# Turning one query block's probabilities with VectorE squares and SBUF transfers in an attention kernel

## What is computed

```
qb = q.reshape(B, H, nb, W, Dh)            # W = 128, nb = 64, H = 16, Dh = 32
kwin = concatenate([kp[:, :, :-2], kp[:, :, 1:-1], kp[:, :, 2:]], axis=3)
vwin = concatenate([vp[:, :, :-2], vp[:, :, 1:-1], vp[:, :, 2:]], axis=3)
scores = einsum('bhnqd,bhnkd->bhnqk', qb, kwin) * scale
scores = where(mask, scores, -1e30)        # |kpos - qpos| <= W and inside the sequence
attn = softmax(scores, axis=-1)
out = einsum('bhnqk,bhnkd->bhnqd', attn, vwin)
return out @ Wout + bout
```

## Time and profile before

| | us |
|---|---|
| median of 3 runs (2625.84 to 2630.6) | 2626.13 |
| the profiled execution | 2629.41 |
| its span, first to last instruction | 2627.6 |
| PE busy in the span | 2576.2 (98%) |
| PE weight loads | 2090.2 (80%) |
| ACT busy | 1638.1 (62%) |
| DVE busy | 1592.0 (61%) |
| POOL busy | 631.8 (24%) |

### The profile page before, as it was taken

The page is one execution under the profiler, slowest core; times in us unless marked ns, Lnnn a source line. Parts: engine busy times, 40 slices in busy tenths (PEclk is TensorE's granted clock), DMA queues, the critical chain, the costliest instruction groups (busy, mean ns, idle before and its releaser), DMA issues.

```text
span 2627.6 us, 55989 instructions
## 1 busy us (share of the span) xinstructions
PE 2576.2 (98%) x19728; PEld 2090.2 (80%) x19728; DVE 1592.0 (61%) x4779; ACT 1638.1 (62%) x4260; POOL 631.8 (24%) x595
## 2 busy tenths in 40 slices
PE   6999999999999999989999999999999999999998
PEld 4888888888888888868888888888888888888885
DVE  5444444444444444357777777777777777777775
ACT  6333333333333333358888888888888888888886
POOL 0011111111111111033333333333333333333332
PEclk7999999999999999999999999999999999999999
DMA  5422222222222222021121111112111111112110
GB/s 181 146 80 81 80 80 80 80 80 80 80 80 80 80 80 64 33 81 34 34 65 34 53 46 42 58 41 58 34 61 39 42 58 42 58 34 65 34 46 29
DMA packets 188361, 167.43 MB, mean 64 GB/s; under 512 B 11328, under 2 KB 143424, under 8 KB 187632
## 3 DMA queue, kind: packets, MB, share of 16 engines
q1 hardware_dynamic: 188000, 164.41, 20.2%
q0 software_dynamic: 144, 0.17, 0.0%
HBM read 97.43 MB, written 67.11 MB: 63 GB/s over the span
## 4 chain that ended last, share of the span: by engine, by line
PE 55%; ACT 1%; issue 0%; DVE 0%; POOL 0%; POOLq 0%; ACTq 0%
PE pT_ps L1193 14%; PE job_ps L1105 14%; PE score_ps L1176 7%; PE job_ps L1123 7%; PE job_ps L1217 7%; PE job_ps L1114 7%; ACT wqkv_raw L928 1%; ACT wqkv_raw L938 0%; PE job_ps L1237 0%; PE score_ps L1227 0%; DVE wqkv_raw L1006 0%; DVE k_lo L1038 0%; ACT q_hi L954 0%; ACT k_hi L957 0%; POOL wout_raw L899 0%
## 5 line engine op out<-in xcount | busy, mean ns | idle before, releaser
L928 ACT ACTIVATE wqkv_raw<-wqkv_raw,neg_max 128x384 f32<-128x384 f32 (+1 forms) x1024 | 633.3, 619 | 186.3 <-DVE neg_max L1006 181.5
L888 POOL TENSOR_SCALAR wqkv_raw<-wqkv_raw,sum_rcp 128x384 f32<-128x384 f32 (+1 forms) x256 | 372.9, 1457 | 960.1 <-DVE sum_rcp L1017 960.1
L494 ACT ACTIVATE relu<-up_ps,fc_scale 128x512 f32<-128x512 f32 x256 | 176.2, 688 | 656.2 <-PE up_ps L625 656.2
L938 ACT COPY wqkv_raw<-pT_ps 128x384 f32<-128x384 f32 (+1 forms) x1024 | 484.7, 474 | 74.4 <-PE pT_ps L1193 74.1
L1193 PE MATMUL pT_ps<-ident,wqkv_raw 128*128 128x128 f32 x3040 | 513.4, 277 | 8.1 <-ACT wqkv_raw L938 7.7
L1006 DVE CUSTOM_DVE_ANT_0 wqkv_raw<-score_ps,mask 128x384 f32<-128x384 f32 (+1 forms) x1024 | 503.5, 548 | 5.7 <-PE score_ps L1176 1.6
L568 DVE SCALAR_TENSOR_TENSOR sq<-up_ps,relu 128x512 f32<-128x512 f32 x256 | 177.0, 692 | 531.8 <-ACT relu L494 530.4
L1193 PEld LDWEIGHTS pT_ps<-ident,wqkv_raw 128*128 128x128 f32 x3040 | 360.0, 140 | 119.1 <-ACT wqkv_raw L938 42.6
L635 PE MATMUL down_ps<-proj_T,sq_hi 128*128 128x512 f32 x1024 | 408.9, 399 | 0.9 <-DVE sq_lo L551 0.9
L637 PE MATMUL down_ps<-proj_T,sq_lo 128*128 128x512 f32 x1024 | 404.3, 395 | 0.0
L621 PE MATMUL up_ps<-f_xT_hi,fc_T 128*128 128x512 f32 x1024 | 399.2, 390 | 1.4 <-DVE low L539 1.4
(11 more groups left out here) (126 smaller groups left out, 4228.2 us busy)
## 6 DMA issues: line engine op xcount, KB each, us to landing
xT_hi<-xT SPq DMA_DIRECT2D x65, 256.0 KB, 3.8
xT_lo<-xT SPq DMA_DIRECT2D x65, 256.0 KB, 4.5
f_x_in<-in_L_attn_x SPq DMA_DIRECT2D x64, 256.0 KB, 3.2
xT<-f_xT_hi SPq DMA_DIRECT2D x64, 256.0 KB, 2.6
xT<-f_xT_lo SPq DMA_DIRECT2D x64, 256.0 KB, 2.8
part_in<-in_L_attn_x SPq DMA_DIRECT2D x64, 256.0 KB, 3.4
partial<-f_y SPq DMA_DIRECT2D x64, 256.0 KB, 2.0
wout_raw<-partial SPq DMA_DIRECT2D x64, 256.0 KB, 2.8
```

The lines of the kernel that those rows point to most:

```text
L888: nc.gpsimd.tensor_scalar(probs[:, u, cols], probs[:, u, cols], sum_rcp[:, u:u + 1], None, ALU.mult).then_inc(last_head_normalised, 1)
L928: nc.scalar.activation(probs[:, u, cols], probs[:, u, cols], ACT.Exp, bias=neg_max[:, u:u + 1], scale=-1.0, accum_out=prob_sum[:, u:u + 1] ...
L938: nc.scalar.copy(pT[:, h, first + seen.start:first + seen.stop, :].rearrange("p w t -> p (w t)"), pT_ps[:, h % 2, seen.start * P:seen.stop ...
```

## The change

For query block 0 of each step the turn leaves PE. Its four heads are scaled by ScalarE (heads 0 and 1) and by GpSimd (heads 2 and 3). VectorE then turns each head by one instruction in 32x32 squares into a new tile `blocks`; a square turned on its own stays in its 32 partitions, so the four strips of 32 partitions have to be carried to where they belong: SP issues 16 transfers SBUF to SBUF a step (4 strips x 4 places), each of 32 partitions x 3 x 128 elements (48 KB in pieces of 512 bytes), into `pT_moved`. `blocks` and `pT_moved` have one buffer each. `probs_times_values` waits for the 16 transfers and multiplies each block on its own, in 24 products of 128 columns where 8 of 256 and 8 of 128 stood. Block 1 goes the old way. To make room, the ring of values has 5 slots (6 before), and that of the attention output 6 steps (8 before). SP's other transfers are issued after the moves of a step.

```diff
+            def move_blocks(t):
+                i, _ = where(t)
+                seen = blocks_seen(i, 0)
+                sp.wait_ge(blocks_turned, HC * (t + 1))
+                if t >= 1:
+                    sp.wait_ge(pv_done, t)
+                for strip in range(STRIPS):
+                    for place in range(STRIPS):
+                        sp.dma_start(pT_moved[place * DH:(place + 1) * DH, seen.start:seen.stop, strip, :, :],
+                                     blocks[strip * DH:(strip + 1) * DH, seen.start:seen.stop, place, :, :]
+                                     ).then_inc(blocks_moved[strip], 16)
...
+            for t in range(STEPS + DC):
+                i, c = where(t)
+                if t < STEPS:
+                    move_blocks(t)
+                if c == 1 and i + XR - 1 < NT:
                     load_x(i + XR - 1)
+                if c >= 2 and i >= 1:
+                    store_y(i - 1, c - 2)
+                    if i < NT:
+                        load_part(i, c - 2)
...
+            def turn_blocks(t, u):
+                i, _ = where(t)
+                seen = blocks_seen(i, 0)
+                if u < HC // 2:
+                    dve.wait_ge(act_heads_normalised, HC // 2 * t + u + 1)
+                else:
+                    dve.wait_ge(pool_heads_normalised, HC // 2 * (t - 1) + u + 1)
+                if u == 0 and t >= 1:
+                    for moved in blocks_moved:
+                        dve.wait_ge(moved, 16 * STRIPS * t)
+                nc.vector.transpose(blocks[:, seen.start:seen.stop, :, u, :].rearrange("p w a t -> p (w a) t"),
+                                    probs[:, u, seen.start * P:seen.stop * P].rearrange("p (b t) -> p b t", t=DH)
+                                    ).then_inc(blocks_turned, 1)
...
                     find_max(t, 0)
-                    normalise(t, 0)
+                    for pair in range(2):
+                        inverse_sums(t, 0, pair)
+                    for u in range(HC // 2):
+                        turn_blocks(t, u)
                 if job_a(t) is not None:
                     qk_low(job_a(t), a_bank(t))
...
                 if t < STEPS:
-                    normalise(t, 1)
+                    for pair in range(2):
+                        turn_blocks(t, HC // 2 + pair)
+                        normalise(t, pair)
...
             def probs_times_values(t):
...
-                pe.wait_ge(pT_done, 8 * t + 2 * HC)
+                for moved in blocks_moved:
+                    pe.wait_ge(moved, 16 * STRIPS * (t + 1))
+                pe.wait_ge(pT_done, HC * (t + 1))
...
                 for part in range(QUARTERS):
-                    if t < STEPS:
-                        turn_probs(t, 0, part)
                     run_b(t, part)
```

More of the change, by code:

```diff
@@ L700, in attention_stage @@
         sum_rcp = sb("sum_rcp", [P, 2 * HC], F32)
-        pT = wqkv_raw[:, 2:4, :].rearrange("p a (h w k) -> p (a h) w k", w=6, k=P)
-        oT_hi = sb("oT_hi", [P, 2, DC, T], F32R)
-        oT_lo = sb("oT_lo", [P, 2, DC, T], F32R)
+        blocks = sb("blocks", [P, 3, STRIPS, HC, DH], F32)
+        pT_moved = wqkv_raw[:, 2, :].rearrange("p (w q h t) -> p w q h t", q=STRIPS, h=HC, t=DH)
+        pT = wqkv_raw[:, 3, :].rearrange("p (h w k) -> p h w k", w=3, k=P)
+        oT_hi = sb("oT_hi", [P, OR, T], F32R)
+        oT_lo = sb("oT_lo", [P, OR, T], F32R)
         part_in = wout_raw[:, 0:2, :]
@@ L725, in attention_stage @@
         normalised, last_head_normalised = sem("normalised"), sem("last_head_normalised")
+        act_heads_normalised, pool_heads_normalised = sem("act_heads_normalised"), sem("pool_heads_normalised")
+        blocks_turned = sem("blocks_turned")
+        blocks_moved = [sem(f"blocks_moved{q}") for q in range(STRIPS)]
         turned = sem("turned")
@@ L929, in exp, with normalise_first_heads, copy_pT @@
                                      accum_out=prob_sum[:, u:u + 1]).then_inc(exped, 1)
-            def copy_pT(t, b, h):
+            def normalise_first_heads(t):
                 i, _ = where(t)
-                seen = blocks_seen(i, b)
-                first = 3 * at(i, b)
-                act.wait_ge(turned, 8 * t + b * HC + h + 1)
+                cols = window(i, 0)
+                act.wait_ge(rcp_done, 4 * t + 1)
+                for u in range(HC // 2):
+                    nc.scalar.mul(probs[:, u, cols], probs[:, u, cols], sum_rcp[:, u:u + 1]
+                                  ).then_inc(act_heads_normalised, 1)
+            def copy_pT(t, h):
+                i, _ = where(t)
+                seen = blocks_seen(i, 1)
+                act.wait_ge(turned, 4 * t + h + 1)
                 if t >= 1:
                     act.wait_ge(pv_done, t)
-                nc.scalar.copy(pT[:, h, first + seen.start:first + seen.stop, :].rearrange("p w t -> p (w t)"),
+                nc.scalar.copy(pT[:, h, seen.start:seen.stop, :].rearrange("p w t -> p (w t)"),
                                pT_ps[:, h % 2, seen.start * P:seen.stop * P]).then_inc(pT_done, 1)
@@ L1001, in find_max @@
                 dve.wait_ge(scored, 2 * t + b + 1)
-                if t >= 1:
-                    dve.wait_ge(turned, 8 * (t - 1) + HC * (b + 1))
+                if t >= 1 and b == 0:
+                    dve.wait_ge(blocks_turned, HC * t)
+                if t >= 1 and b == 1:
+                    dve.wait_ge(turned, HC * t)
                 for h in range(HC):
@@ new lines, in normalise @@
+            def normalise(t, pair):
+                i, _ = where(t)
+                cols = window(i, 1)
+                first = HC + 2 * pair
+                inverse_sums(t, 1, pair)
+                dve.wait_ge(rcp_done, 4 * t + 2 + pair + 1)
+                for u in range(first, first + 2):
+                    if u % HC < HC - 1:
+                        nc.vector.tensor_scalar(probs[:, u, cols], probs[:, u, cols], sum_rcp[:, u:u + 1], None,
+                                                ALU.mult).then_inc(normalised, 1)
@@ L1256, in _ @@
                     if 1 <= t <= STEPS:
-                        turn_probs(t - 1, 1, part)
+                        turn_probs(t - 1, part)
                     run_a(t, part)
```

112 lines of the change are left out of this document (53 added, 59 removed).

## The result

The changed kernel takes 3477.34 us (median of 4 runs, 3474.81 to 3482.52), against 2626.73 for the kernel before in the same session: 1.3237 times as long, with a 95% interval of 1.3214 to 1.326. The forecast was 3072 with a range up to 3460. The direction and the circle of waits were as predicted; the price of handing the squares over was not, and it put the time 17 us above the range.

A forecast was written before the change was run, and what follows sets the result against it. PE was taken to bound the kernel at 11.44 us a step; the new circle of 8.85 us for SP and transfers plus VectorE's part made 14.9, 128 x 3.48 = 445 us more, so 3072 us, range 2820 to 3460.

The forecast's parts named there:

- PE's share: PE's work a step: four head turns go, 1.32 us, values' product unchanged (upper bound +0.72), 11.44 to 10.1 us.
- ScalarE, VectorE: Work they receive: a ScalarE scaling 0.38 us, a VectorE turn 0.48; VectorE's part of the circle 5.97 us.
- The circle: VectorE's first turn waits for the last step's moves, these for its fourth turn; the loop takes 14.9 us a step.
- is more than this late? ... covered: `oT_low` on VectorE: the values' product is ready after 1.9 us, VectorE arrives after 3.8, so no added delay.
- I take the row nearest in pieces: 0.432 + 0.043 = 0.475: SP's issuing of moves: 0.475 us from start to start, 15 issues 7.1 us a step, bounds 5.6 to 10.1.
- The landing: Time from a move's issue until its data has arrived: 1.7 us, bounds 1.3 and 2.8.
- an issue costs what L840's does: Rival: three dimensions set SP's issue at 0.673 us, step 17.9, 3450 us; chance of 3400 or more 0.14.
- a step of 13 to 17.7 us: The main forecast case, moves setting the length of an attention step; chance 0.71.
- the moves hide: Rival: moves cost no time, ScalarE and VectorE's circle of 11.0 us sets the step, 2569 us; faster side's chance 0.09.
- The estimate of 3.8 us: Moves of a step by the skill page's fit, 2.0 us plus all 786 KB at 436 GB/s: 3.8 us.
- The clock: Rival: PE, idle 4.8 us a step, drops to half clock; all work so: 20.2 us a step, 3747 us; chance 0.04.

The follow-up runs named there:

- four_moves: Changed kernel with 4 of the 16 moves a step, all waits kept, part of the result left out: 2658.31 us, ratio 1.0103 to the kernel before.
- two_block_buffers: Changed kernel with two buffers of `blocks`, so VectorE's first turn waits for the moves of the step before the last: 3439.74 us, ratio 1.3073.
- issue_costs: Kernel before, followed by eleven rows of six SBUF to SBUF transfers of different shapes on SP: 32 x 128 took 0.590 us an issue, 128 x 3 x 128 0.644.
- issue_sides: Kernel before, followed by rows of six transfers between SBUF and DRAM in various directions, from SP, ScalarE and GpSimd: 0.42 us with one end in DRAM, 0.59 SBUF to SBUF.
- two_issuers: Changed kernel in the order of turns_together, eight moves issued by SP and eight by GpSimd: 2725.07 us, ratio 1.0358.
- eight_moves: Changed kernel with 8 of the 16 moves a step, all waits kept, part of the result left out: 2818.61 us, ratio 1.0716.
- through_dram: Changed kernel in no_circle's order with contiguous pieces and single buffers, squares carried through DRAM by one store and four loads a step: 2850.31 us, ratio 1.0809.
- contiguous_moves: Changed kernel with both tiles laid out so a move is one run of 384 elements a partition: 3447.98 us, ratio 1.3104.
- turns_together: Changed kernel with all four turns ahead of `find_max` of block 1, one buffer: 3106.56 us, ratio 1.1818.
- no_circle: Changed kernel with two buffers of both tiles, ScalarE's scalings behind `qk_high`, all four turns behind `find_max` of block 1: 3073.75 us, ratio 1.1693.

## Why the prediction went wrong where it did

**PE's share.** Right: 10.28 us a step at full clock (four_moves), 10.1 predicted; the 48 passes take 1.52 us where 32 took 1.44, near the lower bound.

**ScalarE, VectorE.** A turn is 0.57 us long and 0.49 from start to start; 0.48 was taken. A scaling on ScalarE is 0.5 us, not the 0.38 of a copy; it lies off the long circle. VectorE's part was 5.87 for 5.97.

**The circle.** Right, with its place and both waits that were to be seen, in 111 of 111 steps, 5.85 us long. But "is more than this late? ... covered" is too short: the second circle over `oT_low` was not covered by 1.9 us once the product took 2.8, but was as long as the first within about 0.3 us (two_block_buffers). In the kernel after ScalarE's part was done at 2318.05, 0.3 us before VectorE came to `oT_low` at 2318.34. It changed nothing in the forecast and everything in the remedy.

**The issue: the step that failed.** "I take the row nearest in pieces: 0.432 + 0.043 = 0.475". Measured are 0.64, and 0.4 us a step of long issues. That is 10.0 us for 7.1: 2.9 of the 3.1 us that the step was short. The rows of before held no transfer with both ends in SBUF, and the nearest row was sought by pieces, which on a move's 32 partitions make 0.01 us of the price (issue_costs). Where the ends lie makes 0.17 of it in rows of six (issue_sides). The long issues showed in the earlier trace rows only as L840's longest, 2.147 us, and the prediction had no term for them.

**The landing.** 1.95 for 1.7, a further 0.25 us a step, 32 us in all.

**The rival "an issue costs what L840's does"** gave 3450 us with 0.673 an issue. Its number was near, but its reason, the three dimensions, fell: moves of one contiguous run have the same price. It came near because a wrong reason had a number close to the right one, which is luck. Had the prediction weighed it as a bound of an unknown cost and not as a pattern's, the range would have ended higher: both issue and landing were above the middle, and the range was cut at 3460, ten us above the one bound alone. The prediction also calls this range "a step of 13 to 17.7 us", but by its own sum 17.7 us is 3427, and 3460 is 18.0, the step that was measured.

**The rival "the moves hide".** Its circle was 11.0; it is 11.5 to 12.3, since the sum left out the third and fourth turn (four_moves). That circle alone, at 11.65, is longer than the 11.44 of before, so cheap moves would have given no gain: in four_moves PE waits 0.12 us a step for them. A kernel without any wait for moves wasn't run. The sentence of the Trainium skill, "DMA: Bandwidth & Descriptors", section "Issuing engines are not separate DMA queues", that initiating is usually small relative to the DMA itself, does not hold for these transfers: one issue takes 0.6 us and its landing 2.0, 16 issues take 10.2, and initiating on two engines saved 381 us (two_issuers). The estimate of 3.8 us took all 16 moves for one transfer, and its fit stands on that page of the Trainium skill for transfers issued by GpSimd; the moves took 12.0 us on average from the first issue to the last landing. The page's rule to coalesce speaks against the change, and the runs agree: eight moves fewer are 5.1 us less a step (eight_moves), and five transfers through DRAM cost less than 16 (through_dram). But merging pieces within a transfer (contiguous_moves) brings 1%.

**The clock.** It did fall, to 0.80 on average: behind the gap of 5.85 us the product of the values (2314.84 to 2317.55) has a granted clock of 0.50, the 1.2 GHz level, and takes 2.8 us instead of 1.5. In the kernel after nothing on the long circle waits for PE, so this costs nothing, as the prediction said, though only 0.3 us were left; in turns_together and no_circle it stands on the path.

## What to carry to other kernels

Count transfers, not bytes: many small moves on one queue cost the issue each, one after another, and the row to price them by is one with the same kind of memory at both ends. Where the trace has none, every price between the cheapest and the dearest row is open, and the range has to hold the dearest together with the other costs. And before work is moved off the engine that bounds the kernel, add up the circle of the engines that receive it: here that circle took up the whole gain while four moves cost PE only 0.12 us a step.

## What the runs showed of the hardware

- In rows of six of 32 x 384, issuing on SP costs 0.42 us with one end in DRAM and 0.59 with both ends in SBUF or both in DRAM, plus 0.04 to the next (issue_sides). With both ends in SBUF it is 0.59 to 0.64 from 6 to 192 KB (issue_costs). For the move's shape ScalarE as issuer takes 0.62, GpSimd 0.545. A store of the output directly behind a row of moves took 0.59 as well (0.35 before), so part of the price may lie with the transfer ahead; this was not separated.
- Two engines issue side by side at nearly the pace that each has alone: 0.65 and 0.57 us for 0.63 and 0.56 (two_issuers, issue_sides).
- Single issues of 0.9 to 1.8 us came 59 times in 128 steps. Of these, 53 began within 0.3 us of a packet of the queues that load instructions, and all within 0.5; of the other issues 2% did. That is a coincidence in time far beyond chance, but no run tested the cause.
